# Moving the start of a mixture-of-experts stage into the last batch of the attention stage before it

## The chip, the cores and the metric

The kernel runs on one core of one Trainium2 chip. The metric is the device time of one execution in microseconds (us). The engines of the core work on their own instruction streams and meet at semaphores: PE (TensorE, matrix products), DVE (VectorE), ACT (ScalarE), POOL (GpSimd) and SP (which here only issues DMAs).

## What is computed

Two layers of attention and feed-forward over x of 8 batches x 256 tokens x 512 features, each sublayer with a layer norm ahead and a residual sum behind. The change lies between the last two:

```python
# layer 1 attention over a latent context, 16 heads
x = x + _L1_xattn_ref(_layernorm(x), ctx_512, ...)
# layer 1 feed forward: 8 experts with 16 hidden units each, top 2 of 8
def _L1_ffn_ref(x, router_w, down_w, up_w):
    logits = jnp.einsum('bth,eh->bte', x, router_w)
    weights = jax.nn.softmax(logits, axis=-1)
    top_w, top_idx = jax.lax.top_k(weights, K)
    topk_mask = jnp.sum(jax.nn.one_hot(top_idx, E, dtype=x.dtype), axis=-2)
    gate = weights * topk_mask
    h = jnp.einsum('bth,eih->beti', x, down_w)
    a = jax.nn.silu(h)
    expert_out = jnp.einsum('beti,ehi->beth', a, up_w)
    return jnp.einsum('beth,bte->bth', expert_out, gate)
x = x + _L1_ffn_ref(_layernorm(x), L1_ffn_router_w, L1_ffn_down_w, L1_ffn_up_w)
```

## The kernel before

The program is four stages one after the other, each a block: layer 0 attention, layer 0 feed forward, `layer1_attention`, `layer1_experts`. At the end of a block every engine branches out of its own stream and waits for all the others; the first instruction of the next block starts on no engine before the last one of the old block has ended on every engine. x (`X`, `g_x` in the profile) stays in SBUF as 16 tiles of 128 tokens x 512, two tiles (t = 0, 1) to a batch. A matrix product in full precision is made of three passes (`products`, lines 44 to 46) over values that are split into a high part in fp32r and the rest: ACT copies a result as the high part (`..._h`), DVE or POOL subtracts it from the value for the low part (`..._l`). The order of the work on an engine is that of the code: it is written out by hand.

**The attention** (names beginning with `c_`) runs 8 batches of 8 head pairs. For a pair PE makes the scores, DVE the maxima, ACT the exponentials, DVE multiplies these by the inverse sums (L1572, tile `probs`, four tiles of 128x256 for a pair), PE turns them (L1387 into `c_turn`), ACT and DVE split the turned ones (`c_pT_h` L1484, `c_pT_l` L1559), PE multiplies them by the context (`attend`, L1395 to L1397 into `c_bank_b`), ACT and DVE split that (`c_h` L1479, `c_l` L1554), and PE multiplies by VO into `c_acc` (`project_out`). PE works on several pairs at a time. Behind the last pair of the last batch there stands a tail with nothing left to put between its steps: turn the last probabilities, `project_out` of pair 6, `attend` of pair 7, its split, `project_out` of pair 7, and the two additions to x (L1579, `add_output`). Then come the statistics of the two last tiles (`new_stats`, L105 and L107), and on POOL six small instructions (`pool_deviations`, L161 to L171) that make 1/sqrt(variance + eps) of them. Of the seven batches before these, statistics and deviations have been made while a later batch ran. During most of a batch POOL has nothing to do.

**The experts** (names beginning with `d_`) run 8 batches in steps, software-pipelined by hand: batch b is normalised (`d_y`, L1676, by DVE for batch 0 and by POOL for the others), turned by PE (`turn_y`, L1728, 8 transposes into `d_turn`), split by ACT and DVE (`d_yT_h` L1767, `d_yT_l` L1850), multiplied by the expert weights in 24 passes of 256 columns (`hidden_units`, into `d_hidden`), then choice of experts on DVE (from `d_logits` L1819 on), exponentials and SiLU on ACT, the gates on POOL (`d_act_h`, L1795), turned (`d_turn_g`) and multiplied into `d_up`. In PE's program `turn_y(0)` and `turn_y(1)` stand ahead of `hidden_units(0)`. At the start of this block ACT and POOL also split the expert weights (`d_wd_h` L1770 and L1771, `d_wd_l` L1799 and L1801, `d_wu_h` L1781, `d_wu_l` L1810). Their raw values arrived by DMA at the start of the attention block.

## Time and profile before

| | |
|---|---|
| time, median of 3 runs (lowest, highest) | 1076.05 us (1071.77, 1076.82) |
| time of the profiled execution | 1067.52 us |
| its span, first to last instruction | 1065.6 us |
| mean granted TensorE clock | 0.976 |
| busy: PE / DVE / ACT / POOL | 92% / 71% / 61% / 31% of the span |
| attention's last addition to x ends | 995.76 us |
| first instructions of the experts' block | 1000.57 us |
| the experts' block to the end of the span | 65.0 us |

The profile is of one execution, and its times are counted from its first instruction. It was 8.5 us faster than the median of the runs without a profile, so differences are taken inside the profile and then applied to the median. A row of a timeline gives the start, the time and the engine of one instruction or of a few merged ones, and in brackets how long the engine had been idle before it and what ended the wait.

### The profile page before, as it was taken

The page shows a single profiled execution, that of the slowest core. Times are in us where ns is not written, and L with a number is a line of the kernel's source. Part 1 is how long each engine was busy: PE and PEld are TensorE (multiplying, and loading weights), DVE is VectorE, ACT ScalarE, POOL GpSimd, SP SyncE. Part 2 cuts the span into 40 slices and gives each one's busy share as a digit, 9 for nine tenths or more (in the row PEclk, how much of TensorE's full clock was granted, in tenths as well). Part 3 has the DMA queues.
Part 4 walks back from the last instruction along what each step waited for, and adds up shares of the span by engine and source line. Part 5 has one row for each costly group of instructions (what it writes and reads, how often), then busy time and mean ns, then how long its engine had stood idle before and what let it go on. Part 6 is the DMA issues. An engine that isn't in the chain of part 4 may idle for free. (4 is left out here: it accounts for less than half of the span.)

```text
span 1065.6 us, 20165 instructions
## 1 busy us (share of the span) xinstructions
PE 982.8 (92%) x7516; PEld 774.5 (73%) x7516; DVE 757.1 (71%) x1646; ACT 646.3 (61%) x1700; POOL 325.4 (31%) x381
## 2 busy tenths in 40 slices
PE   5889999998479999888999999999999999999587
PEld 4678888876335555456888888888888888888475
DVE  5768988787369888167677677676777777676366
ACT  4678888777257877455455555455455455555175
POOL 5766677456343340520020020201002020000572
PEclk9899999999889999989999999999999999999899
DMA  7120121000091000530000000000000000000013
GB/s 276 66 109 2 46 86 41 2 2 2 16 302 59 1 2 1 179 99 1 1 21 1 1 21 1 21 1 2 20 2 21 1 1 1 2 1 2 0 41 119
DMA packets 20128, 41.80 MB, mean 39 GB/s; under 512 B 1216, under 2 KB 4544, under 8 KB 19520
## 3 DMA queue, kind: packets, MB, share of 16 engines
q1 hardware_dynamic: 20032, 40.53, 11.5%
q8 instruction: 60, 0.98, 0.4%
q14 instruction: 36, 0.29, 0.1%
HBM read 36.33 MB, written 4.19 MB: 38 GB/s over the span
## 5 line engine op out<-in xcount | busy, mean ns | idle before, releaser
L1479 ACT ACTIVATE c_h<-c_bank_b 128x512 fp32r<-128x512 f32 x64 | 38.2, 597 | 158.5 <-PE c_bank_b L1397 158.5
L650 POOL TENSOR_TENSOR a_probs<-a_probs,a_inv 128x256 f32<-128x256 f32 (+1 forms) x128 | 110.3, 888 | 69.8 <-DVE a_inv L747 69.5
L1493 ACT ACTIVATE probs<-c_score,c_neg_max 128x256 f32<-128x256 f32 x256 | 119.2, 480 | 9.8 <-DVE c_neg_max L1564 9.7
L513 ACT ACTIVATE a_probs<-a_s,a_neg_max 128x128 f32<-128x128 f32 (+1 forms) x256 | 104.2, 435 | 27.6 <-DVE a_neg_max L735 27.2
L1554 DVE TENSOR_TENSOR c_l<-c_bank_b,c_h 128x512 fp32r<-128x512 f32 x64 | 44.3, 691 | 104.6 <-ACT c_h L1479 104.6
L44 PE MATMUL c_acc<-VO_h,c_l 128*128 128x512 f32 x256 | 101.2, 396 | 1.9 <-DVE c_l L1554 1.9
L1484 ACT ACTIVATE c_pT_h<-c_turn 128x512 fp32r<-128x512 f32 x128 | 69.6, 596 | 50.2 <-PE c_turn L1387 50.2
L45 PE MATMUL c_acc<-VO_l,c_h 128*128 128x512 f32 x256 | 100.0, 391 | 0.0
L46 PE MATMUL c_acc<-VO_h,c_h 128*128 128x512 f32 x256 | 99.9, 390 | 0.0
L1237 POOL TENSOR_TENSOR c_ctx_raw<-c_ctx_raw,c_table 128x1024 f32<-128x1024 f32 x8 | 19.0, 2381 | 229.1 <-PE c_bank_b L1397 212.3
L1564 DVE TENSOR_REDUCE c_neg_max<-c_score 128x2 f32<-128x512 f32 x128 | 81.7, 680 | 0.8
L1559 DVE TENSOR_TENSOR c_pT_l<-c_turn,c_pT_h 128x512 fp32r<-128x512 f32 x128 | 81.8, 680 | 0.0
L161 POOL TENSOR_SCALAR c_var<-g_mean_var 128x2 f32<-128x2 f32 x8 | 1.8, 224 | 257.1 <-DVEq L1585 257.1
L1572 DVE TENSOR_SCALAR probs<-probs,c_inv 128x256 f32<-128x256 f32 x256 | 75.1, 356 | 5.0
L44 PE MATMUL c_bank_a<-c_yT_h,A_l 128*128 128x256 f32 x256 | 77.2, 301 | 0.0
L46 PE MATMUL c_bank_a<-c_yT_h,A_h 128*128 128x256 f32 x256 | 72.1, 282 | 0.0
L45 PE MATMUL c_bank_a<-c_yT_l,A_h 128*128 128x256 f32 x256 | 72.0, 281 | 0.0
L1387 PE MATMUL c_turn<-g_ident,probs 128*128 128x128 f32 x512 | 69.5, 279 | 0.0
L735 DVE TENSOR_REDUCE a_neg_max<-a_s 128x2 f32<-128x256 f32 (+1 forms) x128 | 63.4, 548 | 4.4 <-PE a_s L372 3.9
L1060 POOL TENSOR_SCALAR b_y<-g_x,g_mean_var,g_rstd 128x512 f32<-128x512 f32 x16 | 44.2, 2766 | 66.0 <-DVE b_xq L1093 65.6
L1013 PE MATMUL b_up<-w,b_xqT 128*128 128x512 bf16 x256 | 61.1, 394 | 2.2 <-ACT b_xqT L1053 2.2
L1387 PEld LDWEIGHTS c_turn<-g_ident,probs 128*128 128x128 f32 x512 | 55.1, 140 | 7.8 <-DVE probs L1572 0.3
(246 smaller groups left out, 2928.3 us busy)
## 6 DMA issues: line engine op xcount, KB each, us to landing
w_raw<-in_w SPq DMA_DIRECT2D x8, 1024.0 KB, 5.5
wq<-in_wq SPq DMA_DIRECT2D x1, 4096.0 KB, 22.8
c_ctx_raw<-in_ctx SPq DMA_DIRECT2D x8, 512.0 KB, 3.5
wo<-in_wo SPq DMA_DIRECT2D x1, 4096.0 KB, 13.9
out<-g_x SPq DMA_DIRECT2D x16, 256.0 KB, 2.0
g_x<-in_x SPq DMA_DIRECT2D x7, 512.0 KB, 6.9
wq_raw<-in_wq SPq DMA_DIRECT2D x4, 256.0 KB, 5.0
a_ctx_raw<-in_ctxT SPq DMA_DIRECT2D x8, 128.0 KB, 3.0
```

Source lines behind the costliest of these rows:

```text
L44: pe.matmul(out, ll, rh, start=start and n == 0, stop=False)
L45: pe.matmul(out, lh, rl, start=False, stop=False)
L46: last = pe.matmul(out, lh, rh, start=False, stop=stop and n == len(pairs) - 1)
L513: last = act.activation(probs[i % 2][:, 2 * pair + j, at], s[:, 2 * pair + j, at], ACT.Exp, bias=neg_max[:, pair, q, j:j + 1], accum_out=s ...
L650: last = pool.tensor_tensor(p, p, inv[:, pair, q, :].unsqueeze(2).broadcast_to([P, 2, (q + 1) * P]), ALU.mult)
L735: last = dve.tensor_reduce(neg_max[:, pair, q, :], s[:, 2 * pair:2 * pair + 2, q * P:(2 * q + 1) * P], AX.X, ALU.max, negate=True)
L1387: last = pe.transpose(turn[k][:, hq * P:(hq + 1) * P], probs[p % 2][:, hq, k * P:(k + 1) * P], ident[:, :])
L1484: act.activation(pT_h[:, k, :], turn[k][:, :], ACT.Copy).then_inc(turn_hi, 1)
L1493: last = act.activation(probs[p % 2][:, i, :], score[h][:, t, :], ACT.Exp, bias=neg_max[:, i:i + 1], accum_out=sums[:, i:i + 1])
L1559: dve.tensor_tensor(pT_l[:, k, :], turn[k][:, :], f32(pT_h[:, k, :]), ALU.subtract).then_inc(turn_lo, 1)
L1564: dve.tensor_reduce(neg_max[:, 2 * h:2 * h + 2], score[h][:, :, :], AX.X, ALU.max, negate=True).then_inc(maxed, 1)
L1572: last = dve.tensor_scalar(probs[p % 2][:, i, :], probs[p % 2][:, i, :], inv[:, i:i + 1], None, ALU.mult)
```

## The change

While the last attention batch runs, POOL normalises batches 0 and 1 of the experts (into y0 and y1), and subtracts for the low parts of the expert weights; ACT copies their high parts; in the tail PE turns batch 0 into the two banks of PSUM in which the scores stood (`score[0]`, `score[1]`), and ACT and DVE split it from there. The buffers for it lie in SBUF where A_h and A_l lay, which nothing reads after the last projection (POOL waits for that with `a_made`). The statistics of the two last tiles are made by DVE at the start of the experts' block, and their deviations by POOL behind the normalisation of batch 4. The experts' block begins with `turn_y(1)`.

```diff
@@ layer1_attention, POOL @@
                 deviations(B - 2)
-                deviations(B - 1)
+                def normalise_first(b):
+                    for t in range(TPB):
+                        tile = b * TPB + t
+                        last = pool.tensor_scalar(first_y[b][:, t, :], X[:, tile, :], mv[:, tile, 0:1], rstd[:, tile:tile + 1],
+                                                  ALU.subtract, ALU.mult)
+                    last.then_inc(first_y_ready, 1)
+
+                wd, wu, _ = expert_raw
+                pool.wait_ge(a_made, a_no(B - 1, LASTP - 1, "proj") + 1)
+                normalise_first(0)
+                for i, cols in enumerate((slice(0, G + E), slice(G + E, S))):
+                    pool.wait_ge(wd_hi, i + 1)
+                    pool.tensor_tensor(wd_l[:, :, cols], wd[:, :, 0:cols.stop - cols.start], f32(wd_h[:, :, cols]), ALU.subtract)
+                normalise_first(1)
+                pool.wait_ge(wu_hi, 1)
+                pool.tensor_tensor(wu_l, wu[:], f32(wu_h), ALU.subtract)
@@ layer1_attention, PE @@
                 transpose_probs(B * PAIRS - 1, LASTP % 2)
+                pe.wait_ge(first_y_ready, 1)
+                for t in range(TPB):
+                    for c in range(DC):
+                        last = pe.transpose(score[t][:].rearrange("p a s -> p (a s)")[:, c * P:(c + 1) * P],
+                                            first_y[0][:, t, c * P:(c + 1) * P], ident[:, :])
+                    last.then_inc(first_turned, 1)
                 project_out(end, LASTP - 1, b_no(end, LASTP, "pv", True))
@@ layer1_attention, ACT @@
                 all_slots(slots)(act)
+                wd, wu, _ = expert_raw
+                act.wait_ge(expert_in, 3 * DMA)
+                act.activation(wd_h[:, :, 0:G + E], wd[:], ACT.Copy).then_inc(wd_hi, 1)
+                act.activation(wd_h[:, :, G + E:S], wd[:, :, 0:S - G - E], ACT.Copy).then_inc(wd_hi, 1)
+                act.activation(wu_h, wu[:], ACT.Copy).then_inc(wu_hi, 1)
                 split_probs(B * PAIRS - 1)
+                for t in range(TPB):
+                    act.wait_ge(first_turned, t + 1)
+                    act.activation(first_yT_h[:, t, :, :].rearrange("p c t -> p (c t)"), score[t][:].rearrange("p a s -> p (a s)"),
+                                   ACT.Copy).then_inc(first_hi, 1)
                 split_context(b_no(B - 1, LASTP, "pv", True) + 1)
@@ layer1_attention, DVE @@
                 split_probs(B * PAIRS - 1)
+                for t in range(TPB):
+                    dve.wait_ge(first_hi, t + 1)
+                    dve.tensor_tensor(first_yT_l[:, t, :, :].rearrange("p c t -> p (c t)"),
+                                      score[t][:].rearrange("p a s -> p (a s)"),
+                                      f32(first_yT_h[:, t, :, :]).rearrange("p c t -> p (c t)"), ALU.subtract)
                 split_context(b_no(B - 1, LASTP, "pv", True) + 1)
                 add_output(B - 1)
-                dve.drain()
-                for t in range(TPB):
-                    new_stats(B - 1, t)
@@ layer1_experts @@
-        steps = range(-3, B + 1)
+        steps = range(-2, B + 1)
@@ layer1_experts, POOL @@
-                normalise(1)
-                pool.wait_ge(wd_hi, 1)
-                pool.tensor_tensor(wd_l[:, :, 0:GE], wd[:], f32(wd_h[:, :, 0:GE]), ALU.subtract).then_inc(wd_lo, 1)
...
+                pool.memset(power[:, :], -0.5)
                 for s in steps:
                     if 0 <= s < B:
                         apply_gates(s)
                     if 2 <= s + 4 < B:
                         normalise(s + 4)
-                    if s == -2:
-                        pool.wait_ge(wu_hi, 1)
-                        pool.tensor_tensor(wu_l[:], wu[:], f32(wu_h[:]), ALU.subtract).then_inc(wu_lo, 1)
+                    if s == 0:
+                        pool.wait_ge(measured, 1)
+                        pool_deviations(pool, mv, rstd, var, sq, power, slice(TILES - TPB, TILES))
@@ layer1_experts, DVE @@
-                normalise_y(dve, 0).then_inc(y0_ready, 1)
+                for t in range(TPB):
+                    dve.bn_stats(last_stats[:, t, :], X[:, TILES - TPB + t, :])
+                dve.drain()
+                for t in range(TPB):
+                    last = dve.bn_aggr(mv[:, TILES - TPB + t, :], last_stats[:, t, :])
+                last.then_inc(measured, 1)
```

The next two pieces are POOL's rows from the deviations of the next-to-last batch's end to the first gates of the experts, of the kernel before and of the changed one. The branches stand where one block ends and the next begins; `d_y0` and `d_y1` are the two buffers for normalised batches.

```order
L171 TENSOR_TENSOR g_rstd<-g_rstd,c_sq 128x2
L1317 UNCONDITIONAL_BRANCH
L1783 UNCONDITIONAL_BRANCH
L1676 TENSOR_SCALAR d_y1<-g_x,g_mean_var,g_rstd 128x512 x2
L1799 TENSOR_TENSOR d_wd_l<-g_wd,d_wd_h 128x4x136
L1801 TENSOR_TENSOR d_wd_l<-g_wd,d_wd_h 128x4x120
L1676 TENSOR_SCALAR d_y0<-g_x,g_mean_var,g_rstd 128x512 x2
L1810 TENSOR_TENSOR d_wu_l<-g_wu,d_wu_h 128x512
L1676 TENSOR_SCALAR d_y1<-g_x,g_mean_var,g_rstd 128x512 x2
L1795 TENSOR_TENSOR d_act_h0<-d_act_h0,d_gate0 128x256
```

```order
L1352 TENSOR_SCALAR d_y0_6844<-g_x,g_mean_var,g_rstd 128x512 x2
L1361 TENSOR_TENSOR d_wd_l_6849<-g_wd,d_wd_h_6848 128x4x136
L1361 TENSOR_TENSOR d_wd_l_6849<-g_wd,d_wd_h_6848 128x4x120
L1352 TENSOR_SCALAR d_y1_6845<-g_x,g_mean_var,g_rstd 128x512 x2
L1364 TENSOR_TENSOR d_wu_l_6851<-g_wu,d_wu_h_6850 128x512
L1320 UNCONDITIONAL_BRANCH
L1807 UNCONDITIONAL_BRANCH
L1821 MEMSET d_power 128x2
L1710 TENSOR_SCALAR d_y0_6844<-g_x,g_mean_var,g_rstd 128x512 x2
L1710 TENSOR_SCALAR d_y1_6845<-g_x,g_mean_var,g_rstd 128x512 x2
L1819 TENSOR_TENSOR d_act_h0<-d_act_h0,d_gate0 128x256
```

Five groups of POOL's rows now stand ahead of the block's end instead of behind it, the deviations that stood there are gone from that place, and two normalisations (of batches 2 and 3) are left ahead of the first gates.

The next two pieces are ACT's rows at the same place, before and changed, from the copy of pair 6's context on.

```order
L1479 ACTIVATE c1_h_7103<-c_bank_b 128x512
L1484 ACTIVATE c_pT_h<-c_turn0 128x512
L1484 ACTIVATE c_pT_h<-c_turn1 128x512
L1479 ACTIVATE c1_h_7103<-c_bank_b 128x512
L1317 UNCONDITIONAL_BRANCH
```

```order
L1504 ACTIVATE c1_h_7111<-c_bank_b 128x512
L1557 ACTIVATE d_wd_h_6848<-g_wd 128x4x136
L1558 ACTIVATE d_wd_h_6848<-g_wd 128x4x120
L1559 ACTIVATE d_wu_h_6850<-g_wu 128x512
L1509 ACTIVATE c_pT_h<-c_turn0 128x512
L1509 ACTIVATE c_pT_h<-c_turn1 128x512
L1563 ACTIVATE d_yT_h0_6846<-c_score0 128x512
L1563 ACTIVATE d_yT_h0_6846<-c_score1 128x512
L1504 ACTIVATE c1_h_7111<-c_bank_b 128x512
L1320 UNCONDITIONAL_BRANCH
```

The three weight copies stand ahead of the split of the last probabilities, and the two copies of the turned batch 0 behind it.

## Rows read from the trace of the kernel before

**Rows 1.** Busy time by stretch: us, PE, PEld, DVE, ACT, POOL, granted clock, DMA, GB/s
```profile
999.00:1000.00 1.00, 0.00 (x0) 0.00 (x0) 0.00 (x0) 0.00 (x0) 0.55 (x4) 0.54 0.00 0
1000.00:1010.00 10.00, 5.59 (x28) 5.22 (x29) 3.11 (x4) 3.72 (x5) 9.58 (x7) 0.53 0.00 0
```

**Rows 2.** Chain that ended last, start of the experts' block: start, us, what
```profile
1000.59 1.30 DVE d_y L1676 x2
...
1006.38 1.94 PE d_turn L1728 x8
...
1011.71 0.17 DVE d_logits L1819
```

**Rows 3.** Timeline of DVE in the last attention batch and its end
```profile
976.40 1.14 DVE L1572 TENSOR_SCALAR probs<-probs,c_inv 128x256 f32<-128x256 f32 x4
...
986.05 1.28 DVE L1559 TENSOR_TENSOR c_pT_l<-c_turn,c_pT_h 128x512 fp32r<-128x512 f32 x2
...
995.07 0.69 DVE L1579 TENSOR_TENSOR g_x<-g_x,c_acc 128x512 f32<-128x512 f32 x1 [0.68 <-PE c_acc L46]
...
997.45 0.18 DVE L107 BATCH_NORM_AGGREGATE g_mean_var<-c_stats 128x2 f32<-128x6 f32 x1
```

**Rows 4.** Timeline of POOL, from the end of attention on
```profile
997.74 0.22 POOL L161 TENSOR_SCALAR c_var<-g_mean_var 128x2 f32<-128x2 f32 x1 [29.96 <-DVEq L1585]
...
999.99 0.19 POOL L171 TENSOR_TENSOR g_rstd<-g_rstd,c_sq 128x2 f32<-128x2 f32 x1
1000.61 4.38 POOL L1676 TENSOR_SCALAR d_y<-g_x,g_mean_var,g_rstd 128x512 f32<-128x512 f32 x2 [0.42 <-POOLq L1317]
1004.96 1.33 POOL L1799 TENSOR_TENSOR d_wd_l<-g_wd,d_wd_h 128x544 fp32r<-128x544 f32 x1
...
1018.09 0.62 POOL L1795 TENSOR_TENSOR d_act_h<-d_act_h,d_gate 128x256 f32<-128x256 f32 x1 [1.15 <-DVE d_gate L1842]
...
1024.25 0.62 POOL L1795 TENSOR_TENSOR d_act_h<-d_act_h,d_gate 128x256 f32<-128x256 f32 x1 [1.42 <-DVE d_gate L1842]
```

**Rows 5.** Timeline at the block boundary behind layer 0's feed forward
```profile
436.62 0.18 DVE L107 BATCH_NORM_AGGREGATE g_mean_var<-b_stats 128x2 f32<-128x6 f32 x1
...
437.07 0.11 POOL L1251 MEMSET c_all_power<- 128x16 f32 x1 [37.54 <-POOLq L986]
```

**Rows 6.** Timeline of PE in the attention's tail and the first expert steps
```profile
979.54 1.09 PE L1387 MATMUL c_turn<-g_ident,probs 128*128 128x128 f32 x8
...
984.62 1.09 PE L1387 MATMUL c_turn<-g_ident,probs 128*128 128x128 f32 x8
986.19 0.50 PE L44 MATMUL c_acc<-VO_h,c_l 128*128 128x512 f32 x1 [0.47 <-DVE c_l L1554]
...
989.04 0.40 PE L1395 MATMUL c_bank_b<-c_pT_h,c_kv_l 128*128 128x512 f32 x1
...
1001.94 1.97 PE L1728 MATMUL d_turn<-g_ident,d_y 128*128 128x128 f32 x8 [6.92 <-DVE d_y L1676]
...
1011.63 1.09 PE L1728 MATMUL d_turn<-g_ident,d_y 128*128 128x128 f32 x8
1012.48 0.36 PE L44 MATMUL d_hidden<-d_wd_h,d_yT_l 128*128 128x256 f32 x1
...
1015.32 0.28 PE L46 MATMUL d_hidden<-d_wd_h,d_yT_h 128*128 128x256 f32 x1
```

**Rows 7.** Timeline of ACT in the tail and the expert steps
```profile
985.31 1.09 ACT L1484 ACTIVATE c_pT_h<-c_turn 128x512 fp32r<-128x512 f32 x2
...
1000.57 0.66 ACT L1770 ACTIVATE d_wd_h<-g_wd 128x544 fp32r<-128x544 f32 x1 [9.34 <-PEq L1317]
...
1027.94 0.38 ACT L1761 ACTIVATE d_g_h<-d_turn_g 128x256 fp32r<-128x256 f32 x1
```

**Rows 8.** One line's instructions (ns min/median/max), and one group of POOL (us, mean ns)
```profile
L1572 DVE TENSOR_SCALAR probs<-probs,c_inv x256: 336/348/693, 479.3 to 984.2; 128x256 f32<-128x256 f32 x128
...
L1060 POOL TENSOR_SCALAR b_y<-g_x,g_mean_var,g_rstd 128x512 f32<-128x512 f32 x16 | 44.2, 2766 | 66.0 <-DVE b_xq L1093 65.6
```

More of the change, by code:

```diff
@@ L1216, in _, with layer1_attention @@
                                       ALU.subtract).then_inc(A_lo, 1)
-def layer1_attention(nc, io, X, mv, rstd, ident, store, ahead, ahead_in, expert_raw, expert_in):
+def layer1_attention(nc, io, X, mv, rstd, ident, store, ahead, ahead_in, expert_raw, expert_in, first):
     with Memory(nc, "c") as m:
@@ L1286, in layer1_attention @@
         outed, added, measured = m.sem("outed"), m.sem("added"), m.sem("measured")
+        first_y, first_yT_h, first_yT_l, wd_h, wd_l, wu_h, wu_l = first
+        first_y_ready, first_turned, first_hi, wd_hi, wu_hi = (
+            m.sem(n) for n in ("first_y_ready", "first_turned", "first_hi", "wd_hi", "wu_hi"))
         vo_made, vo_hi, vo_lo = m.sem("vo_made"), m.sem("vo_hi"), m.sem("vo_lo")
```

55 lines of the change are left out of this document (22 added, 33 removed).

## The prediction, made before the changed kernel ran

> **What bounds the kernel now.** I read the busy time by stretch first, to see where PE, the busiest engine, stands still. Between 1000 and 1010 us, the first ten microseconds of the experts' block, PE is busy 5.59 us, at a granted clock of 0.53, while POOL is busy 9.58; in the slice before, PE did nothing at all [rows 1]. The reader is to see a hole between two stages. The chain that ended last tells what fills it: DVE normalises batch 0 from 1000.59, PE turns it at 1001.94, after the splits PE turns batch 1 at 1006.38, and only at 1011.71 does DVE read the first logits [rows 2, 6]. The timelines of DVE and POOL tell what lies ahead of it: the last addition to x ends at 995.07 + 0.69 = 995.76, then come the statistics, to 997.63, and POOL's deviations from 997.74 to 1000.18, about 0.4 us of block change, and the first experts' instructions at 1000.57 to 1000.61 [rows 3, 4, 7]. From the last addition to the first logits it is 1011.71 - 995.76 = 15.95 us, all of it on the path. From there the experts run as a ring: one batch's gates follow the last one's by 1024.25 - 1018.09 = 6.16 us [rows 4]. Nothing there changes but one piece of POOL work, so the question is what the 15.95 us become.
>
> **The changed path, step by step.**
>
> *PE's extra transposes in the tail.* Eight of them start one after the other in 1012.48 - 1011.63 = 0.85 us at full clock [rows 6]. The last probabilities' own eight start at 984.62, so PE is free at 985.47, stands until 986.19 for `c_l`, and starts `project_out` there [rows 6]. The added eight take 985.47 to 986.32: 0.13 us beyond. From below the cost is 0.13, from above 1.09 (the whole group with its pipeline end) less the free time that the row itself shows, 0.47, thus 0.62. I take 0.2, nearer the pace of starts, since PE pipelines them.
>
> Is y0 ready then? POOL is released by the last projection, whose split precedes DVE's multiplication at 976.40 in DVE's program. 976.40 + 4.38 (two 128x512 on POOL) = 980.8, against 985.47 [rows 3, 4, 6]. Cover 4.7 us.
>
> *ACT's three weight copies* stand ahead of the last probabilities' split, which starts at 985.31 now. At 0.66 each at most, 1.98 us [rows 7]. DVE's `c_pT_l`, both halves done at 986.05 + 1.28 = 987.33, is then done by 989.3, the first half 0.6 earlier. `attend` reads the first half at 989.04 + 0.2, the second three products later [rows 3, 6]. So it costs nothing, but with a few tenths of cover; the bound above is 0.3. The two copies of batch 0 and their subtractions (two 128x512 on each engine, as the probabilities' 1.09 and 1.28, [rows 3, 7]) fall into the time of `attend`, when both engines wait.
>
> *POOL's share.* The weight parts can start at 985.31 + 0.66 = 985.97. Three subtractions of at most 1.33 and batch 1's 4.38 are 8.37: done at 994.3, ahead of the last addition's end at 995.96 [rows 3, 4, 7]. Cover 1.6 us. If POOL's normalisation goes at the 2.77 us per tile that it took in layer 0's feed forward [rows 8] it is 2 x 2.77 - 4.38 = 1.2 us more, still inside.
>
> *The block change.* Behind the last DVE instruction of the feed-forward stage the next block begins after 437.07 - 436.80 = 0.27 us [rows 5]; here it was about 0.4. I take 0.35: the experts start at 995.96 + 0.35 = 996.3 instead of 1000.57.
>
> *First logits.* PE now does `turn_y(1)` and `hidden_units(0)` at once, with nothing to wait for. The same pair of groups ran from 1011.63 to 1015.32 + 0.28 = 1015.60, 3.97 us at full clock [rows 6]. 996.3 + 4.0 = 1000.3 for the end of `hidden_units(0)`, and 1000.3 for the logits against 1011.7: **11.4 us** earlier. DVE's statistics, now here, need 997.63 - 995.76 = 1.9 us and stand only ahead of batch 1's low part, which waits for PE's turn (0.9) and ACT's copy (1.0) in any case. Batch 2's normalisation on POOL ends at 996.3 + 0.1 + 4.4 = 1000.8, batch 3's at 1005.2. The first gates come 1018.09 - 1011.71 = 6.4 us behind the logits, at 1006.7 [rows 2, 4]: 1.5 us of cover.
>
> *The deviations on POOL in the ring.* They are 1000.18 - 997.74 = 2.44 us, once. A step of POOL is 0.62 + 4.38 = 5.0 of the 6.16 us, so the second gates are up to 2.44 - 1.16 = 1.3 us late [rows 4]. PE turns them, and ACT reads the turned ones at 1027.94, 3.07 us after POOL's end at 1024.87 [rows 4, 7]; POOL gets 1.16 back in the next step. I take nothing; the bound above is 1.3.
>
> *PE's clock.* The granted clock was 0.54 on average between 999 and 1000, so it fell from 2.4 to 1.2 GHz at about 999.1, when PE had been idle since 1001.94 - 6.92 = 995.02 [rows 1, 6]. The eight transposes then took 1.97 us instead of 1.09. In the changed kernel PE is idle from about 995.2 to 996.3 only. I expect full clock, and 3.97 us is counted so. At the lower clock throughout, starts lie twice as far apart: 3.97 becomes at most 7.9, and with a clock that comes back halfway, as it did here in 1000 to 1010, about 2.5 us are lost.
>
> **Sum.** 11.4 us less. In the profile: span 1065.6 to 1054.2, its own time 1067.52 to 1056.1. The median of the three runs is 8.5 us above the profiled time, which nothing in the profile explains; I subtract the saving from it: 1076.05 - 11.4 = **1064.7 us**.
>
> **A rule on the shared port.** Where DVE and POOL meet in the trace, DVE loses little: of the 256 multiplications of `probs` the median took 348 ns and the longest 693, with POOL at work beside some of them, and DVE's two tiles of d_y took 1.30 us while POOL's ran for 4.38 [rows 2, 4, 8]. POOL, for its part, took 2.77 us a tile in the feed forward [rows 8]. Four multiplications lengthened by 0.35 are 1.4 us; the pair at 976.40 ends at 977.54 and PE reads it at 979.54, so 2.0 us cover it [rows 3, 6]. The Trainium skill, "SBUF — State Buffer", section "Who interferes with whom", says that DVE and GpSimd share a port pair, that whoever issues first holds it for the whole instruction and the other fully blocks. By that rule the sum would hold an extra 2.4 us at most, by the rows above nothing; d_y's 1.30 beside 4.38 speaks against it, as two instructions of 2 us should have kept DVE off.
>
> **The rivals.**
>
> *POOL holds DVE off in the last batch.* y0's two instructions would keep the multiplications from 976.40 until 980.78; PE, which is the bound there, would get them at 981.9 instead of 979.54, 2.4 us late. 1064.7 + 2.4 = 1067.1. The 693 ns show a wait of only 0.35 us [rows 8]. Chance 0.06.
>
> *The clock falls in spite of the short gap.* 2.5 us are lost at the start: 1067.2. For it speaks that the tail has holes of its own; against it that the clock was still full 4 us into the old gap. Chance 0.07.
>
> *The change does not do what it says: POOL carries the boundary.* If its four pieces behind 985.97 take double, 16.7 us, the block changes at 1002.7 instead of 996.0, and 6.7 of the 11.4 us are gone: 1071.4, inside what a measurement can tell from no change. It would take twice the durations of [rows 4] where the worst row has 1.3 times. With smaller losses that add up, chance 0.09.
>
> *Slower: the ring becomes POOL's.* From batch 4 on POOL reads x and writes the y tiles at their new addresses. Up to a step of 6.16 us POOL costs nothing, and at 2 x 2.77 + 0.62 = 6.16 it is just at that point. Over the six steps that still have a normalisation it eats the gain from 6.16 + 11.4 / 6 = 8.1 us a step on, and is slower by over 0.5% from 9.0. At 9.5 the time is 1064.7 + 6 x 3.3 = 1084.7. Nothing in the trace has POOL at 4.4 us a tile. Chance 0.03.
>
> **How the numbers follow.** My forecast, a gain of 9.5 to 12.5 us, has 0.75, and its own range is 1061.5 to 1067. The bounds of the unknown costs are +0.4, +0.3 and +1.3 us, the two rivals near 1067 end the same way, and three runs of one kernel lay between 4.3 us below and 0.8 us above their median. So the range is 1060 to 1069, which leaves out POOL at the boundary and the slower case and a little of the scatter. A measurement of this kernel tells about 0.5%, 5.4 us, from no change. Faster by more: 0.75 + 0.06 + 0.07 = 0.88; the same: 0.09; slower: 0.03.
>
> **What would show it.** In the changed profile: no DVE or POOL work between the last addition and the block change, and that gap under 0.5 us; PE's first transposes in the experts at full clock, the first logits some 4 us behind the block change, and the first gates 6.4 us behind those; `project_out` of pair 6 late by under 0.6 us; POOL idle at the end of the attention block for 1 to 2 us; the second gates up to 1.3 us late with nothing behind them late; the step at 6.16 us. I am wrong if the block change waits for POOL, if the multiplications of `probs` under y0 are above 0.7 us each, if the clock column of the first expert slices is near 0.5, or if the logits come early and the ring then waits for POOL's y tiles.

## The result and the profile after

The changed kernel took **1057.97 us** (median of 4 runs, 1057.33 to 1060.71), the kernel before 1075.87 on the same chip (4 runs). By the medians it is 17.9 us faster, where 11.4 were predicted and the range ended at 1060. The ratio of the runs is 0.9846, 95% interval 0.9815 to 0.9876, which is 16.6 us of 1075.87 (13.3 to 19.9). The profiled execution took 1060.71 us, its span is 1058.6 us, its mean granted clock 0.974. The busy time of POOL is 31% of the span as before, and that of PE 93%.

The stretches that answer to [rows 1], and one with the products of the next-to-last batch, are these in the profile after (us from the span's start, length, then PE, PEld, DVE, ACT and POOL busy, the granted clock, DMA share, GB/s):

```profile
999.00:1000.00 1.00, 0.16 (x2) 0.19 (x3) 0.68 (x2) 0.00 (x0) 0.20 (x2) 1.00 0.00 0
1000.00:1010.00 10.00, 7.70 (x64) 7.29 (x63) 6.87 (x21) 5.50 (x9) 8.13 (x4) 1.00 0.01 2
...
1048.00:1052.00 4.00, 2.59 (x6) 2.07 (x7) 1.97 (x6) 0.89 (x3) 0.62 (x1) 0.68 0.35 131
```

PE is busy 7.70 of the block's first ten microseconds instead of 5.59, at a granted clock of 1.00 instead of 0.53. The hole is gone. In the last row six products ran at the lower clock, after PE had waited 2.56 us for DVE. In the profile of before PE waited as long at this place (2.55 us), and the clock stayed full:

```profile
1057.90 0.50 PE L44 MATMUL d_up<-d_wu_h,d_g_l 128*128 128x512 f32 x1 [2.55 <-DVE d_g_l L1861]
```

So the wait is not new; the fall of the clock behind it is. The timeline of DVE in the changed kernel answers to [rows 3] and to the logits of [rows 2]:

```profile
980.00 1.65 DVE L1606 TENSOR_SCALAR probs<-probs,c_inv 128x256 f32<-128x256 f32 x4
...
991.08 1.29 DVE L1593 TENSOR_TENSOR c_pT_l<-c_turn,c_pT_h 128x512 fp32r<-128x512 f32 x2 [1.35 <-ACT c_pT_h L1509]
...
998.84 0.69 DVE L1613 TENSOR_TENSOR g_x<-g_x,c_acc 128x512 f32<-128x512 f32 x1 [0.69 <-PE c_acc L46]
999.84 1.29 DVE L1865 BATCH_NORM_STATS2 d_last_stats<-g_x 128x6 f32<-128x512 f32 x2 [0.32 <-PEq L1320]
...
1003.81 0.17 DVE L1838 COPY d_logits<-d_hidden 128x16 f32<-128x16 f32 x1 [0.59 <-PE d_hidden L46]
```

The last addition ends at 999.53, the first instruction of the experts starts at 999.80, and the first logits are read at 1003.81: 4.28 us, where it was 15.95. POOL's timeline answers to [rows 4]:

```profile
978.28 4.28 POOL L1352 TENSOR_SCALAR d_y<-g_x,g_mean_var,g_rstd 128x512 f32<-128x512 f32 x2 [6.90 <-PE c_bank_a L46]
989.63 2.55 POOL L1361 TENSOR_TENSOR d_wd_l<-g_wd,d_wd_h 128x544 fp32r<-128x544 f32 x2 [7.08 <-ACT d_wd_h L1557]
992.16 4.14 POOL L1352 TENSOR_SCALAR d_y<-g_x,g_mean_var,g_rstd 128x512 f32<-128x512 f32 x2
996.26 1.29 POOL L1364 TENSOR_TENSOR d_wu_l<-g_wu,d_wu_h 128x512 fp32r<-128x512 f32 x1
999.80 0.10 POOL L1821 MEMSET d_power<- 128x2 f32 x1 [2.25 <-POOLq L1320]
999.89 8.24 POOL L1710 TENSOR_SCALAR d_y<-g_x,g_mean_var,g_rstd 128x512 f32<-128x512 f32 x4
1010.03 0.62 POOL L1819 TENSOR_TENSOR d_act_h<-d_act_h,d_gate 128x256 f32<-128x256 f32 x1 [1.90 <-DVE d_gate L1861]
...
1017.53 0.62 POOL L1819 TENSOR_TENSOR d_act_h<-d_act_h,d_gate 128x256 f32<-128x256 f32 x1 [0.21 <-issue]
...
1022.66 0.62 POOL L1819 TENSOR_TENSOR d_act_h<-d_act_h,d_gate 128x256 f32<-128x256 f32 x1 [0.35 <-DVE d_gate L1861]
```

POOL had ended its share of the change at 997.55, 2.0 us ahead of the last addition's end. The second gates come 7.50 us behind the first, 1.3 late, and the third 5.13 behind these. PE's and ACT's timelines answer to [rows 6, 7]:

```profile
988.22 1.09 PE L1406 MATMUL c_turn<-g_ident,probs 128*128 128x128 f32 x8
989.15 1.04 PE L1483 MATMUL c_score<-g_ident,d_y 128*128 128x128 f32 x8
...
999.84 1.06 PE L1757 MATMUL d_turn<-g_ident,d_y 128*128 128x128 f32 x8 [1.04 <-PEq L1320]
1000.66 0.36 PE L44 MATMUL d_hidden<-d_wd_h,d_yT_l 128*128 128x256 f32 x1
...
1049.41 0.80 PE L44 MATMUL d_up<-d_wu_h,d_g_l 128*128 128x512 f32 x1 [2.56 <-DVE d_g_l L1885]
1050.00 0.63 PE L45 MATMUL d_up<-d_wu_l,d_g_h 128*128 128x512 f32 x1
```

```profile
988.41 0.60 ACT L1504 ACTIVATE c_h<-c_bank_b 128x512 fp32r<-128x512 f32 x1 [1.68 <-PE c_bank_b L1416]
```

This last row is ACT's copy of pair 6's context, the last instruction ahead of anything that the change touches. In [rows 7] it has no row; in the profile of before it starts at 984.81. **The changed kernel came 3.6 us later to the change, and its stretch from there on was 70.19 us instead of 80.79.** I divide every profile at this copy from here on ("the mark"); ahead of it both kernels run the same instructions, but for POOL's first piece, which lies in POOL's idle time. It did not move the mark: from DVE's multiplications under it (976.40 before, 980.00 after) to the mark it is 8.41 us in both.

### The profile page after: what moved, and what is told of

Its sections match the earlier page's. It is cut to its first block and busy times, and to the rows that moved or that the text cites. A ratio compares the mean times of both kernels' runs of the same rounds, so it can differ in the third digit from the quotient of the medians.

```text
span 1058.6 us, 20162 instructions
## 1 busy us (share of the span) xinstructions
PE 985.2 (93%) x7516; PEld 774.4 (73%) x7516; DVE 756.7 (71%) x1645; ACT 646.0 (61%) x1701; POOL 329.8 (31%) x384
## 3 DMA queue, kind: packets, MB, share of 16 engines
q1 hardware_dynamic: 20032, 40.53, 11.5%
## 5 line engine op out<-in xcount | busy, mean ns | idle before, releaser
L1022 PE MATMUL b_down<-w,b_hqT 128*128 128x512 bf16 x256 | 59.5, 387 | 1.5 <-ACT b_hqT L1038 1.5
```

## Experiments

The steps behind the mark, in us, each a difference of two starts or ends in the profile named. "Batches 2 to 8" goes from the first gates to the last. I call an execution early when its mark comes at 987.5 or before, and late otherwise. e1 to e4, and the kernel before beside them, ran on another chip than c, d, f and g; its median there was 1075.89 (17 runs).

| profile | mark at | to last addition's end | block change | to first logits | to first gates | batches 2 to 8 | to the end | mark to end |
|---|---|---|---|---|---|---|---|---|
| before | 984.81 | 10.95 | 4.81 | 11.14 | 6.38 | 40.41 | 7.10 | 80.79 |
| c1, before again | 990.53 | 10.93 | 4.81 | 12.17 | 6.11 | 41.15 | 8.50 | 83.67 |
| after | 988.41 | 11.12 | 0.27 | 4.01 | 6.22 | 39.98 | 8.59 | 70.19 |
| c2, after again | 991.73 | 11.12 | 0.28 | 4.01 | 6.22 | 40.00 | 8.54 | 70.17 |
| c3, only statistics | 990.39 | 10.99 | 0.28 | 10.99 | 6.63 | 40.03 | 8.39 | 77.31 |
| c4, statistics stay | 988.65 | 11.13 | 4.87 | 5.80 | 6.43 | 40.46 | 10.66 | 79.35 |
| d1, warm end | 991.66 | 11.09 | 0.27 | 4.01 | 6.23 | 40.03 | 7.11 | 68.74 |
| d3, warm gap | 985.12 | 10.99 | 4.81 | 10.90 | 6.63 | 40.44 | 7.11 | 80.88 |
| e1, before, busy | 990.86 | 10.96 | 4.81 | 12.45 | 5.99 | 39.83 | 7.10 | 81.14 |
| e2, after, busy | 990.94 | 11.08 | 0.28 | 4.01 | 6.22 | 41.35 | 7.12 | 70.06 |
| e3, weights stay | 989.37 | 11.09 | 0.30 | 8.83 | 5.98 | 40.07 | 7.06 | 73.33 |
| e4, both turned | 991.01 | 11.12 | 0.27 | 3.19 | 6.31 | 40.00 | 7.10 | 67.99 |
| g1, best, prelude busy | 985.93 | 11.12 | 0.27 | 3.19 | 6.30 | 39.89 | 7.10 | 67.87 |
| g2, best, plain | 991.64 | 11.12 | 0.27 | 3.18 | 6.32 | 41.36 | 7.11 | 69.36 |

In c4's "to the end" 4.66 us lie behind the last addition to x, where the profiles without a pad have 2.4 to 2.5: its last two stores took 3.4 us to land instead of 2.0. This is left out below.

| run | median us (lowest, highest, runs) | ratio to before, 95% interval |
|---|---|---|
| c1 | 1074.18 (1067.72, 1077.70, 12) | 0.9983 (0.9959, 1.0007) |
| c2 | 1058.51 (1057.40, 1063.95, 7) | 0.9839 (0.9820, 0.9857) |
| c3 | 1069.37 (1067.99, 1069.75, 6) | 0.9938 (0.9921, 0.9955) |
| c4 | 1068.17 (1064.79, 1071.16, 6) | 0.9927 (0.9903, 0.9951) |
| d1 | 1062.46 (1059.41, 1064.04, 6) | 0.9897 (0.9863, 0.9931) |
| d2 | 1070.56 (1065.96, 1073.89, 12) | 0.9960 (0.9935, 0.9984) |
| d3 | 1069.66 (1067.42, 1073.88, 12) | 0.9969 (0.9944, 0.9994) |
| d4 | 1077.54 (1072.98, 1084.09, 12) | 1.0047 (1.0014, 1.0079) |
| e1 | 1074.29 (1072.33, 1075.87, 12) | 0.9995 (0.9979, 1.0011) |
| e2 | 1061.97 (1061.33, 1063.06, 6) | 0.9879 (0.9859, 0.9899) |
| e3 | 1065.48 (1064.91, 1066.40, 6) | 0.9913 (0.9893, 0.9933) |
| e4 | 1060.21 (1059.83, 1061.91, 5) | 0.9861 (0.9839, 0.9883) |
| f1 | 1060.62 (1057.45, 1063.62, 6) | 0.9866 (0.9833, 0.9899) |
| f2 | 1079.55 (1070.75, 1080.80, 12) | 1.0025 (0.9995, 1.0055) |
| f3 | 1084.83 (1076.75, 1087.37, 12) | 1.0090 (1.0060, 1.0119) |
| f4 | 1062.03 (1061.30, 1067.37, 6) | 0.9895 (0.9861, 0.9929) |
| g1 | 1055.87 (1054.44, 1056.87, 5) | 0.9816 (0.9789, 0.9843) |
| g2 | 1062.48 (1061.78, 1062.95, 5) | 0.9876 (0.9849, 0.9902) |

### c1 and c2: both kernels again, unchanged

> The kernel before, unchanged, timed against itself and profiled once more. Path theory (the change is worth what the tail's path says, 10 to 12 us, and the rest of the 17.9 us between the medians is scatter of the stages ahead, where the profiled execution happened to be 8.5 us faster than the median): the same block as ever from the attention's last addition to the end, 15.95 us to the first logits, and any difference of the new profile from 1065.6 us lies before 980 us. Rival (the old experts' block itself runs slower when it is not profiled): the new profile, if it is of a slow execution, has the extra time behind 995 us. Ratio 1.00 by both.

> The changed kernel, on the same chip and in the same rounds as the kernel before. Path theory: 10 to 12 us less than the kernel before if both are in the same scatter of the stages ahead. Rival: 17 to 18 us less again, and then the path in the tail does not hold the whole gain.

c2 is 17.3 us below the kernel before beside it (1075.83): the number of the rival. The scatter is large and one-sided. In 109 executions of the kernel before, all groups of runs together, the median is 1075.68 us; 61 took 1075 or more and only 15 under 1070. **The execution that was profiled for the prediction, 1067.52, was an early one.** The second profile of the same program shows where the time lies (stretches, columns as above, first of the profile of before, then of c1):

```profile
250.00:260.00 10.00, 8.95 (x92) 7.18 (x90) 7.32 (x16) 7.34 (x25) 5.54 (x6) 1.00 0.01 4
...
490.00:500.00 10.00, 9.55 (x59) 7.78 (x60) 6.78 (x14) 4.70 (x13) 0.00 (x0) 1.00 0.00 0
```

```profile
250.00:260.00 10.00, 8.95 (x74) 6.78 (x74) 5.14 (x11) 5.86 (x21) 4.59 (x6) 0.69 0.00 1
...
490.00:500.00 10.00, 8.35 (x31) 4.32 (x30) 5.36 (x13) 4.39 (x10) 0.00 (x0) 0.83 0.00 0
```

In such stretches the granted clock fell from 2.4 to 1.2 GHz in one execution (0.69 and 0.83 of full on average) and stayed full in the other, with the same instructions. The mark comes at 984.81 in one and at 990.53 in the other. So 5.7 us of the difference lie ahead of the mark, where the path theory puts all of it. Behind it the late execution loses 2.9 us more, which is the rival's place: 1.03 to the first logits, 0.74 in batches 2 to 8, 1.40 at the end, less 0.27 between logits and gates. Two padded late executions of the kernel before (f2 and d4, marks 991.90 and 991.68) have the same 83.7 us when the pad is taken off, and an early one that stands between (f3, mark 987.33) has 82.3. The changed kernel's stretch depends far less on it: 70.19, 70.17, and 70.13 in f1, with marks from 988.41 to 991.73, and 70.4 in d2, whose mark is at 985.34.

### c3 and c4: the statistics alone, and everything but the statistics

c3 is the kernel before with one part of the change:

```diff
@@ layer1_attention, POOL and DVE @@
-                deviations(B - 1)
...
-                    new_stats(B - 1, t)
@@ layer1_experts, DVE and POOL @@
+                    dve.bn_stats(last_stats[:, t, :], X[:, TILES - TPB + t, :])
...
+                        pool_deviations(pool, mv, rstd, var, sq, power, slice(TILES - TPB, TILES))
```

c4 is the changed kernel with exactly that part taken back.

> One part alone: the statistics and deviations of the last two tiles go into the experts' block, nothing else moves (the batches' normalisation, the turning and the weight split stay where they were). Path theory: the block changes 0.3 us behind the last addition instead of 4.8, all behind it as before: 4.5 us less than before, logits still 11.1 us behind the block change. Rival (any kernel with changed code sheds some 6 us that do not lie on this path): about 11 us less.

> The other part alone: the changed kernel, with the statistics and deviations put back at the end of the attention block. Path theory: 11.4 - 4.5 = 6.9 us less than before, and up to 2.5 less than that if PE's clock falls in the gap of 5.7 us that PE then has: 4.5 to 7. Rival of a common 6 us: 11 to 13 us less.

The medians are 6.5 us (c3) and 7.7 us (c4) below the kernel before beside them, where 4.5 and 4.5 to 7 were expected; the rival of a common 6 us, 11 and more in each, did not come. Up to the last gates (the sum without "to the end") before has 73.69 us, c3 68.92, c4 68.69 and after 61.60. So the statistics alone are worth 4.8, the rest alone 5.0, and together they are worth 12.1. Most of the missing 2.3 is the clock's. In c4 PE's turning is 5.59 us behind its last work and runs at the lower clock, and so do the first products behind it:

```profile
1004.65 1.94 PE L1761 MATMUL d_turn<-g_ident,d_y 128*128 128x128 f32 x8 [5.59 <-PEq L1320]
```

From block change to logits it takes 5.80 us instead of 4.01. Short gap and short start help each other.

### d1: PE kept busy in the last steps

```diff
+                    for n in range({6: 18, 7: 5}.get(s, 0)):
+                        pe.transpose(turn[:, n % 2, n // 2 % DC, :], ident[:, :], ident[:, :])
```

> The changed kernel, with 18 idle transposes on PE behind the gates' turn of batch 6 and 5 behind that of batch 7, into a PSUM tile that nothing reads any more. Theory (in the changed kernel PE's clock falls in the last step, where the six products of the last but one batch took 2.6 us instead of 1.4): the stretch from the last gates to the end comes down from 8.5 to about 7.1 us, as it was in the profile of before, and the whole is 1.0 to 1.5 us below the changed kernel. Rival (the end is bound by ACT and DVE, the clock does not matter there): no change.

```profile
1049.96 2.13 PE L1770 MATMUL d_turn<-g_ident 128*128 128x128 f32 x18
1052.69 0.50 PE L44 MATMUL d_up<-d_wu_h,d_g_l 128*128 128x512 f32 x1 [0.60 <-DVE d_g_l L1887]
```

With 18 transposes in the wait the products behind it take 0.39 us, not 0.63, and the last gates are 7.11 us from the end instead of 8.59. All six profiles with these transposes (d1, e2, e3, e4, g1, g2) have 7.1 us there. Of the fourteen without them, pads taken off, three have it (before, d3, e1), in the others the clock fell in the last batches. So the lower clock is the loss, and the transposes kept it away wherever they stood; why the same wait is harmless in some executions is not shown. The median is higher than the changed kernel's all the same: 5 of its 6 executions took 1061.9 us or more, where its mark is at 991.66. A median of this program says nothing about 1.5 us.

### d3: the clock held up in the old gap

The kernel before, with transposes in both halves of the gap:

```diff
                 project_out(end, LASTP, b_no(end, LASTP, "pv", True) + 1)
+                for n in range(44):
+                    pe.transpose(bank_a[:, n % 4 * P:(n % 4 + 1) * P], ident[:, :], ident[:, :])
@@ layer1_experts, PE @@
+                for n in range(10):
+                    pe.transpose(turn_g[:, n % 4 * P:(n % 4 + 1) * P], ident[:, :], ident[:, :])
```

> The kernel before, with idle transposes on PE across the change of blocks (44 behind its last product of the attention, 10 ahead of its first turn in the experts), so that it stands still for less than a microsecond at a time. Theory (part of the gain of the change is the clock that no longer falls there): block change to first logits in 8.5 to 9 us instead of 11.1 to 12.2, so 2 to 3.5 us below the kernel before. Rival (the clock is not what is short there): no change, or slower by the idle transposes.

The clock was 1.00 from 999 to 1000 (it was 0.54), and nothing came of it in the profile, which is of an early execution: 80.88 us. One reason is POOL, which normalises batch 1 and then splits the weights:

```profile
1000.97 4.38 POOL L1678 TENSOR_SCALAR d_y<-g_x,g_mean_var,g_rstd 128x512 f32<-128x512 f32 x2 [0.42 <-POOLq L1317]
1005.32 1.33 POOL L1803 TENSOR_TENSOR d_wd_l<-g_wd,d_wd_h 128x544 fp32r<-128x544 f32 x1
1006.62 1.20 POOL L1805 TENSOR_TENSOR d_wd_l<-g_wd,d_wd_h 128x480 fp32r<-128x480 f32 x1
```

```profile
1007.96 0.55 PE L44 MATMUL d_hidden<-d_wd_h,d_yT_l 128*128 128x256 f32 x1 [0.44 <-POOL d_wd_l L1805]
```

POOL's split was the last thing that PE waited for, by 0.44 us. The other reason is that the clock fell again, behind PE's wait of 2.46 us for batch 0's low part:

```profile
1006.00:1009.00 3.00, 2.56 (x13) 2.19 (x13) 0.39 (x1) 1.44 (x2) 3.00 (x3) 0.53 0.03 5
```

The runs tell more than the profile. The ratio is 0.9969, some 3.3 us, and the slowest runs of d3 took 1073.9 where the slowest of before take 1077 to 1078. This fits the 2.9 us that a late execution of before loses behind the mark, though no late execution of d3 was profiled.

### d2, d4, f2, f3, f4: pads behind the end, and f1

```diff
+                @block.gpsimd
+                def _(pool):
+                    pool.memset(rest[:], 0.5)
+                    pool.drain()
+                    for _ in range(7):
+                        pool.tensor_tensor(rest[:], rest[:], rest[:], ALU.mult)
+                        pool.drain()
```

Each adds such a block behind the old end, with 2, 4 or 7 multiplications (3.3, 5.7 and, by these two, 9.2 us): d2 (7) and f4 (2) behind the changed kernel, f2 (2), d4 (4) and f3 (7) behind the kernel before. f1 is the changed kernel again.

> The changed kernel and behind it a block in which POOL alone works for some 10.5 us, so that the program is as long as the one before. Theory that the stages ahead depend on the length of the whole program (executions follow one another, and the clock's changes fall elsewhere in the next one): the executions scatter as those of before do, and the median is 14 to 17 us over the changed kernel, close to that of before. Rival (what is ahead of the change doesn't depend on it; the whole difference lies behind the last attention batch): the median is 10.5 us over the changed kernel, and most executions lie within 2 us of the fastest.

> The kernel before and behind it a block in which POOL alone works for some 6 us. Theory that the length of the program matters for its stages ahead: a median that is not 6 us over the one before but up to 8 us less or 2 more, and other spans than 1065.7, 1071, 1073.7 and 1075 plus 6. Rival: the median is 6 us over the one before, with the same scatter.

> The changed kernel as it is, for the share of its executions that come early to the change (up to now 8 of 11 have a time of 1058.96 us or less, and 3 have 1060.7 to 1064.0). Theory P (the share follows the length of the program or the sequence of executions, not the changed code): any share, but the early executions at 1057 to 1059 again and the late ones 3 to 6 us above. Theory C (the changed code makes the stages ahead of it faster): again about three quarters early.

> The kernel before, and behind its last block one more in which POOL does two multiplications (some 3 us in all). Nothing ahead of the old end is touched. Taking the 3 us off, theory C expects the spread of the kernel before, 1068 to 1078 with a median near 1076 and few executions below 1070; theory P another share of early ones than before's (about 12 in 74 below 1070 us), as with the pad of 5.7 us, where 6 of 12 were.

> The same with seven multiplications (some 9 us in all). Theory C: 1084 to 1085 as the median, few below 1079. Theory P: a share of early ones (below 1079) that differs from before's and from that of the shorter pads.

> The changed kernel with the pad of two multiplications (some 3 us). Theory C: three quarters of the executions at 1060 to 1062, as the changed code's share goes with it. Theory P: a share unlike that, as with the pad of seven, where 5 of 12 were early.

Early by the rule above are, pads taken off, executions of the kernel before of 1071.4 us or less and of the changed kernel of 1059.5 or less. Side by side it looks like this:

| runs beside each other | kernel before | before with a pad | changed kernel | changed with a pad |
|---|---|---|---|---|
| the first result | 0 of 4 | | 3 of 4 | |
| c (before with c1) | 4 of 29 | | 5 of 7 | |
| d | 10 of 28 | 6 of 12 (d4) | | 5 of 12 (d2) |
| e (other chip), g | 2 of 17, 0 of 8 | | | |
| f | 9 of 23 | 4 of 12 (f2), 5 of 12 (f3) | 3 of 6 (f1) | 4 of 6 (f4) |

The kernel before itself went from 4 of 29 to 9 of 23 between two groups of runs, with nothing changed. Beside that a pad made no difference that such numbers can tell (9 of 23 and 9 of 24 in f). d2 is 12 us above the changed kernel of c and not 9.2, and its runs spread over 8 us, against its rival; but f1, without a pad, had only 3 of 6 early too, not three quarters. So neither theory P (length or sequence) nor theory C (the changed code) is shown. Whether the changed kernel comes early more often stays open: it did in the first two groups (8 of 11 against 4 of 33) and not clearly in f (3 of 6 against 9 of 23).

### e1 and e2: PE kept busy ahead of the change, in both kernels

```diff
+                    keep_busy(out, {("pv", B - 1, 2): 42, ("pv", B - 1, 3): 4, ("out", B - 1, 0): 10}.get((kind, b, i), 0))
...
+                for n in range(170):
+                    pe.matmul(up[:, 0:P], identb[:, :], identb[:, :], start=True, stop=True)
...
+                        for k in range(22 if n == 2 else 6):
+                            pe.transpose(banks[0][:, k % 4 * P:(k % 4 + 1) * P], ident[:, :], ident[:, :])
```

> The kernel before, with transposes of the identity matrix (nobody reads them) put into PE's waits ahead of the change's place: 22 and 6 ahead of two score steps of the last batch of layer 0's attention, 42, 4 and 10 in its tail, 170 at the start of layer 0's feed forward, 24 and 12 in its last two steps, and 6 to 22 ahead of each turned part of the score weights. Where the granted clock falls in these waits is the only difference that I found between executions of one kernel ahead of the change. Theory A (the clock's falls ahead of the change make the scatter, and the profiled execution of before was one of the few with the mild ones): the last context of pair 6 is split at 984 us or earlier in the profile, against 985 to 992 up to now, the runs lie within 3 us of each other, and the median is 1061 to 1068. Theory B (the scatter has another source, DMA or the engines' start): the median is within 3 us of before's 1076 and the runs still spread over 5 us. Either way the profile's stretch from pair 6's context to the end is 80.8 to 83.7 us as in the kernel before.

> The changed kernel with the same transposes upstream, and with the transposes at the end of the experts that took the clock's fall out of the last step. Both kernels then come to the change in the same state, so that the difference of this one and the one beside it is what the change itself is worth together with the end's 1.4 us. Theory A: the stretch from pair 6's context to the end is 68.7 us, the difference to the kernel before with the same transposes is 12.1 us when that one's stretch is 80.8 and 14.9 when it is 83.7, and the time is 1049 to 1055 with runs within 3 us. Theory B (about 4 us of the 17.9 between the medians are really the change's, by some effect on the stages ahead): the difference is 16 us or more although the stretches differ by 12 to 15.

The scatter is nearly what theory A expected (3 us): 12 runs of e1 lie within 3.5 us and 6 of e2 within 1.7, while the kernel before beside them had 8.1. The level is not: e1's 1074.29 is where theory B had it. The marks are at 990.86 and 990.94, not at 984, since layer 0's feed forward (its first normalisation to the attention block's start) now took 152.4 us instead of 147.4. But both kernels have it alike, and their medians differ by 1074.29 - 1061.97 = **12.3 us**, the theory's 12.1. This is what the change is worth, together with the transposes at the end, when both kernels come to it alike. (Their profiles differ by 11.1: in e2's the clock fell once more, from 1022 to 1026, and batches 2 to 8 took 1.4 us more than in e4's.)

### e3: the weights' split stays in the experts

e2 with ACT's three copies and POOL's three subtractions back at the experts' start.

> The last kernel with one part of the change undone: ACT copies the expert weights' high parts, and POOL subtracts for the low parts, at the start of the experts' block again, while batches 0 and 1 are still normalised and batch 0 turned in the attention. Theory A (the path through the start is a chain of waits as the prediction adds it up): hidden_units(0) waits for POOL's second part, which ends some 0.7 + 1.3 + 1.3 = 3.3 us behind the block change, instead of 1.0; the first logits come 2.3 us later, POOL's normalisation of batch 3 then ends up to 0.8 us behind the first gates' inputs, and the time is 2.3 to 3.1 us longer. Rival (POOL is so lightly loaded that the split hides behind the turned batch 1): under 0.7 us longer.

```diff
@@ layer1_experts, POOL @@
+                for i, cols in enumerate((slice(0, GE), slice(GE, WIDTH))):
+                    pool.wait_ge(wd_hi, i + 1)
+                    pool.tensor_tensor(wd_l[:, :, cols], wd[:, :, 0:cols.stop - cols.start], f32(wd_h[:, :, cols]), ALU.subtract
+                                       ).then_inc(wd_lo, 1)
```

It costs 3.5 us by the medians, more than either theory said. POOL's second part is late by what was expected, and then PE's clock goes:

```profile
1001.00:1004.00 3.00, 0.84 (x8) 0.61 (x6) 2.38 (x5) 2.42 (x4) 2.50 (x3) 0.86 0.00 0
1004.00:1009.00 5.00, 4.94 (x23) 4.94 (x24) 0.17 (x1) 0.00 (x0) 5.00 (x5) 0.50 0.00 0
```

PE waits 2.21 us for `d_wd_l`, and the products behind the wait run at half clock: 8.83 us to the logits, not 6.3.

### e4, g1 and g2: batch 1 turned in the tail too

```diff
                 attend(B * PAIRS - 1, end % 2, b_no(end, LASTP, "pv", True) + 1)
+                pe.wait_ge(first_y_ready, 2)
+                for t in range(TPB):
+                    for c in range(DC):
+                        last = pe.transpose(turn[t][:, c * P:(c + 1) * P], first_y[1][:, t, c * P:(c + 1) * P], ident[:, :])
+                    last.then_inc(first_turned, 1)
```

Its splits stand behind that of the last context, and POOL normalises both batches before it turns to the weights. e4 has e2's busy waits, g1 only those ahead of the parts of the score weights, g2 none ahead of the experts.

> The changed kernel with the same transposes, taken one step further: batch 1 is turned and split in the attention's tail too, behind the last attend and ahead of the last project_out, where PE waits for the context's split; POOL normalises batches 0 and 1 first and then subtracts for the weights. The experts begin with hidden_units(0) and no turning. Theory A: behind the block change the first logits come 3.1 us later instead of 4.0; the eight transposes cost 0.1 to 0.5 us in the tail; the stretch from pair 6's context to the end is 68.0 to 68.4 us, the time 0.3 to 0.8 us below the last but one. Rival: the second copies on ACT and subtractions on DVE (1.1 and 1.3 us) hold up the last addition to x or POOL's longer run ahead of the weights carries the block's end, and nothing or less than nothing is gained (68.7 or more).

> The kernel with both batches turned in the attention's tail and transposes at the end of the experts, and of the transposes upstream only those around the turned parts of the score weights; those in layer 0, which made the stage before the attention 4 to 5 us longer, are gone. Theory: the stretch from pair 6's context to the end stays 68.0 us, or 66.5 if a fall of the clock behind the second gates stays away; the stretch from the attention block's start to pair 6's context is 545.5 to 547.2 us against 547.7 to 549.7 in kernels without these transposes; so the time is 1053 to 1060 us with a median of 1055 to 1058, below the changed kernel's 1058.5. Rival: the transposes ahead of the score weights' parts cost as much as the clock gives back, and the next kernel is as fast or faster.

> The same without any transposes ahead of the experts. Theory: stretch to the end as in the last, the stages ahead as scattered as in the changed kernel: early executions at 1055 to 1056, late ones at 1060 to 1062; against the last one slower in the late executions by 2 to 3 us.

The first logits come 3.19 us behind the block change instead of 4.01, and the tail did not grow (11.12). g1 is the best version, 1055.87 us, 5 runs within 2.4; g2 has the same instructions from the attention's first batch on and is 6.6 us slower by the medians, and slower than the changed kernel although its stretch behind the mark is 0.8 us shorter. All its executions came late. What g1 keeps busy (window columns as above):

```profile
450.00:460.00 10.00, 9.93 (x69) 6.07 (x68) 2.91 (x4) 6.13 (x11) 5.26 (x4) 1.00 0.90 338
460.00:470.00 10.00, 9.63 (x71) 7.99 (x70) 6.21 (x10) 5.59 (x10) 0.00 (x0) 1.00 0.29 83
490.00:500.00 10.00, 8.90 (x56) 6.88 (x55) 7.10 (x16) 5.30 (x14) 0.00 (x0) 1.00 0.01 2
```

The same stretches of g2:

```profile
450.00:460.00 10.00, 7.44 (x38) 2.47 (x35) 2.19 (x3) 6.50 (x11) 6.77 (x5) 1.00 1.02 382
460.00:470.00 10.00, 6.76 (x33) 5.50 (x32) 4.47 (x8) 4.18 (x7) 0.00 (x0) 0.60 0.13 31
490.00:500.00 10.00, 8.35 (x28) 4.46 (x29) 5.81 (x13) 4.96 (x15) 0.00 (x0) 0.83 0.00 0
```

From the attention block's start to the mark g1 takes 545.5 us and g2 549.7, as both were expected to. The 6.6 us between them are more than the expected 2 to 3: the clock fell once more behind g2's second gates, 1.5 us, and one more lies ahead of the attention block.

## Why the prediction was wrong

**The path was right.** PE's transposes in the tail were to cost 0.2 and ACT's copies nothing; the tail grew by 0.17 in all. The block change was put at 0.35 and took 0.27. The first logits were to come 3.97 us behind it and came 4.01. The gates were to follow after 6.4 and did after 6.22. The second gates were to be up to 1.3 us late with nothing lost: 1.34 late, and all of it back one batch later. The step stayed at 6.16 to 6.17. POOL's cover at the boundary was to be 1.6 us and was 2.0. None of the rivals came as it was told: the clock stayed at 1.00 over the block change, POOL did not carry the boundary, and the ring did not become POOL's.

**The shared port.** DVE's four multiplications beside POOL's y0 took 1.65 us instead of 1.14, and POOL's two instructions 4.28. They lost 0.51 us, inside their cover of 2.0. These are the first of them and POOL's first instruction, then three multiplications of the kernel before, of which the first ran beside another POOL instruction:

```profile
978.28 2.09 POOL L1352 TENSOR_SCALAR d_y<-g_x,g_mean_var,g_rstd 128x512 f32<-128x512 f32 x1 [6.90 <-PE c_bank_a L46]
980.00 0.51 DVE L1606 TENSOR_SCALAR probs<-probs,c_inv 128x256 f32<-128x256 f32 x1
```

```profile
553.69 1.29 POOL L1243 TENSOR_TENSOR c_kv_l<-c_ctx_sum,c_kv_h 128x512 fp32r<-128x512 f32 x1
554.45 1.20 DVE L1572 TENSOR_SCALAR probs<-probs,c_inv 128x256 f32<-128x256 f32 x3
```

The prediction read "DVE loses little" from the longest of the 256 multiplications, 693 ns. Only six of the 256 ran beside a POOL instruction; these took 678 to 693 ns each and ended 0.15 us behind it, and no other took over 355. As they began when only 0.5 us of the POOL instruction was left, they do not show what a long one costs. The rule of the Trainium skill ("SBUF — State Buffer", "Who interferes with whom"), by which the loser fully blocks, is given there for DVE instructions in a 2-port mode, which a `tensor_scalar` can enter; no row tells the mode. By their ends these six, and the first multiplication under y0, which ended 0.15 us behind POOL's first instruction, can have been held off until POOL had ended. The other three were not: they ended by 981.65, while POOL's second ran from 980.35 to 982.56. So the rule is neither shown nor refuted here, and the prediction's ground for setting it aside was too thin; that the loss stayed inside its cover is in part luck.

**The step that failed** is the one of the sum: "The median of the three runs is 8.5 us above the profiled time, which nothing in the profile explains; I subtract the saving from it". The profile is of an early execution, the median that of late ones, and neither the saving nor the stages ahead are the same in the two:

- In early executions the stretch behind the mark went from 80.79 to 70.4 us (d2), a gain of 10.4: 11.5 to the first logits, as predicted, 0.7 more up to the last gates, and 1.8 lost behind them.
- In late ones it went from 83.67 to 70.17, a gain of 13.5. Where the clock was low, a late execution of the kernel before lost 1.5 us more up to the last gates, which the change takes away, and 1.4 behind them. The changed kernel loses these 1.4 too, but in early and late executions alike, so that the late ones are no worse off by them.
- The rest, some 4 us of the 17.9, lies ahead of the change. Before's median execution is a late one and the changed kernel's an early one; their marks must lie 4 to 5 us apart (an estimate from their spans and stretches; no profile is of a median execution). e1 and e2 show by the other way what is left when this is taken out: 12.3 us, or about 10.9 without the transposes at the end.

**One loss was not foreseen:** PE's clock fell at the end of the experts, 8.59 us from the last gates to the end instead of 7.10 in the profile of before. Behind a wait that both kernels have, the products ran at 1.2 GHz, and d1's transposes took this away. Late executions of before have the same loss (8.50), so it is no effect of the change on the medians.

What stays open is why an execution comes early or late, and whether the change has a part in it (11 of 17 against 25 of 109, groups of runs mixed). Its code ahead of the mark is the same but for POOL's first piece. Of the kernels near to it c3, d1 and g2 had no early execution among 17, c4 had 3 of 6. If the share had been that of the kernel before, the median would have been about 1075.7 - 13.5 = 1062.2, an estimate from the two late stretches; that is inside the predicted range.

## What to carry to other kernels

A single profile is one draw. Before a saving read from it is taken off a median, ask which of the executions was profiled: 8.5 us between them was larger than any single term of the sum. Compare the times of several runs, look for stretches in which the granted clock differs at the same instructions, and divide the program at a mark, so that what a change does is told from how its executions arrive. Where the clock falls behind waits of 2 to 3 us in some executions, cheap work for PE in them made the times steady, and gave 4 us where it cost nothing else (g1), but it cost 5 us where it lengthened the stage (e1). A share of early executions that is counted in one group of runs is not to be compared with one of another.

## What the runs showed that I had not expected

- With the same instructions, the start of the attention's last tail came between 984.8 and 992 us. The runs of the kernel before spread over 7 to 10 us in each group of more than four, and those of e1 to e4 and g1, with PE kept busy in the waits ahead, over 1.5 to 3.5 us. (c3 and g2 spread over 1.8 and 1.2 without it, but had late executions only.)
- A wait of 2.2 us for POOL cost 4.8 us at the logits, as the 24 products behind it ran at 1.2 GHz (e3).
- Six multiplications on DVE that ran beside a POOL instruction took 0.68 to 0.69 us, the 250 others of their kind at most 0.355.
- Two parts of the change were worth 4.8 and 5.0 us alone and 12.1 together (c3, c4).
- A kernel with 0.8 us less work behind the mark was 4 us slower by its median (g2 against the changed kernel), through the stages ahead alone.
